# A Mamba cross-attention layer with routed experts: the short convolution on TensorE, and all expert products in plain fp32

## What is computed

```
x   = einsum('ed,bld->bel', in_proj_w, ctx)                 # 256 channels
xc  = depthwise causal conv of x, 4 taps per channel
u   = silu(xc + conv_b)
dt, B, C = split(x_proj_w @ u);  delta = softplus(dt_proj_w @ dt + dt_proj_b)
state = state * exp(delta * A) + (delta * u) * B            # 16 states, 256 steps
y   = (sum over states of state * C + D * u) * silu(layernorm(input))
x1  = input + tanh(g0) * y
h   = silu(hn @ wg[e].T) * (hn @ wu[e].T), hn = layernorm(x1)   # 10 experts, 176 wide
out = x1 + tanh(g1) * (shared + 2.5 * top-2 weighted sum of h @ wd[e].T)
```

## Time and profile before

| | us |
|---|---|
| median of 3 runs (lowest, highest) | 253.39 (253.25, 253.78) |
| the profiled execution | 253.55 |
| its span | 251.7 |
| busy PE, DVE, ACT, POOL | 205.5, 215.0, 171.2, 195.3 |

### The profile page before, as it was taken

One profiled execution on the slowest core, in us unless ns is written; L12 is line 12 of the kernel. 1 busy time (PEld: TensorE's weight loads), 2 busy tenths in 40 slices (PEclk: granted clock), 3 DMA queues, 4 the chain that ended last, 5 costly groups with the idle time before them and its releaser, 6 DMA issues. The chain is left out here.

```text
span 251.7 us, 3757 instructions
## 1 busy us (share of the span) xinstructions
PE 205.5 (82%) x874; PEld 148.7 (59%) x874; DVE 215.0 (85%) x522; ACT 171.2 (68%) x508; POOL 195.3 (78%) x237
## 2 busy tenths in 40 slices
PE   8534594658669895677996899889999999999995
PEld 4223273434355662345854587568888778788884
DVE  2789999999998989999999999989999999645340
ACT  4579879997758997458757998676775682343220
POOL 0248889999999999999999999999999996510000
PEclk9855579575979999999999999999999999999999
DMA  6496999770490202002209302020300000000000
GB/s 183 140 263 172 336 410 321 281 230 1 130 364 12 83 21 87 0 16 68 81 14 329 109 0 83 27 83 3 101 3 0 22 3 3 21 0 0 3 21 21
DMA packets 26821, 25.45 MB, mean 101 GB/s; under 512 B 1064, under 2 KB 25904, under 8 KB 26160
## 3 DMA queue, kind: packets, MB, share of 16 engines
q1 hardware_dynamic: 26512, 25.06, 30.7%
q10 hardware_dynamic: 288, 0.16, 0.2%
HBM read 24.04 MB, written 1.18 MB: 100 GB/s over the span
## 5 line engine op out<-in xcount | busy, mean ns | idle before, releaser
L1061 POOL TENSOR_TENSOR dbu<-du,bb 128x512 f32<-128x512 f32 x64 | 81.3, 1284 | 5.1 <-DVE du L463 3.3
L704 ACT ACTIVATE psA<-delta,aneg 128x127 f32<-128x127 f32 x256 | 78.0, 358 | 5.6 <-DVE psH L953 5.3
L953 DVE TENSOR_TENSOR_SCAN psH<-psA,dbu 128x512 f32<-128x512 f32 x64 | 76.5, 1218 | 1.5 <-POOL dbu L1087 0.4
L667 PE MATMUL psU<-wup,hnT 128*128 128x352 f32 x176 | 63.6, 491 | 12.8 <-DVE hcat L869 8.9
L1104 POOL TENSOR_TENSOR acc<-acc,prod 128x512 f32<-128x512 f32 x42 | 54.5, 1297 | 2.4 <-DVE prod L963 1.8
L545 PE MATMUL psD<-wdn,hT 128*128 128x256 f32 x224 | 52.2, 380 | 0.6 <-issue 0.6
L667 PEld LDWEIGHTS psU<-wup,hnT 128*128 128x128 f32 x176 | 32.8, 200 | 32.8 <-DVE hcat L869 13.6
L833 ACT ACTIVATE tg<-psU 128x176 f32<-128x176 f32 x80 | 24.4, 314 | 36.7 <-PE psU L667 23.9
L545 PEld LDWEIGHTS psD<-wdn,hT 128*128 128x128 f32 x224 | 41.5, 190 | 6.7 <-issue 1.1
L963 DVE TENSOR_TENSOR prod<-psH,cc 128x512 f32<-128x512 f32 x64 | 41.9, 679 | 1.1 <-POOL acc L1104 0.7
L1035 DVE SCALAR_TENSOR_TENSOR ag<-tg,psU 128x176 f32<-128x176 f32 x80 | 25.5, 330 | 15.5 <-ACT tg L833 15.1
(11 more groups left out here) (117 smaller groups left out, 282.9 us busy)
## 6 DMA issues: line engine op xcount, KB each, us to landing
cc<-brows SPq DMA_DIRECT2D x16, 512.0 KB, 4.9
bb<-brows SPq DMA_DIRECT2D x3, 2048.0 KB, 7.6
wup<-in_w_up SPq DMA_DIRECT2D x1, 1760.0 KB, 12.2
wdn<-in_w_down SPq DMA_DIRECT2D x1, 1664.0 KB, 16.5
wup<-in_w_up SPq DMA_DIRECT2D x1, 1408.0 KB, 8.4
x_sb<-in_x SPq DMA_DIRECT2D x4, 256.0 KB, 4.2
bb<-brows SPq DMA_DIRECT2D x1, 1024.0 KB, 5.9
out<-outb SPq DMA_DIRECT2D x8, 128.0 KB, 1.7
```

The source lines that it names most:

```text
L667: last = pe.matmul(dst, hnT[:, b % 2, k, lh * P:(lh + 1) * P], wup[:, j - 1, k, :], start=(k == 0), stop=(k == KT - 1))
L704: last = act.activation(dst[:, j, h, 1:], delta[:, b % 2, h, l0 + 1:l1], ACT.Exp, scale=aneg[:, h * DS + s0 + j:h * DS + s0 + j + 1])
L953: dve.tensor_tensor_scan(psH[:, i % 2], psA[:, i % DA_RING], dbu[:, i % DBU_RING], 0.0, ALU.mult, ALU.add).then_inc(s_scan, 1)
L1061: pool.tensor_tensor(tile(dbu[:, m % DBU_RING], m), du[:, b % 2, :, l0:l1].unsqueeze(1).broadcast_to(shape), bb[:, b % 2, s0:s0 + ns, l0:l ...
```

## The change

The short convolution is made on TensorE: for each of the four taps, `win` is scaled by that tap per channel into `wk[:, k]`, and `project` accumulates four products of shifted context in PSUM. The scaling is done once at the start, two taps on VectorE and two on GpSimd (`scale_tap`), from a broadcast of the taps over all partitions that ScalarE's queue loads into two slots of `prod`. `project_out` scales by 0.5 and adds the bias; `tap0` to `tap2` are gone. All units are plain fp32 products; `whi`, `wlo`, `hnhi`, `hnlo` and the tasks that make them are gone. The orders of all engines but SyncE are written anew.

```diff
@@ the tables of units
-SPLIT = ((1, 2), (3, 3), (5, 2), (7, 3), (9, 2))
...
@@ set-up
+        wk = sb("wk", [P, DC, DI])
-        whi = sb("whi", [P, NSPLIT, KT, 2 * FF], F32R)
-        wlo = sb("wlo", [P, NSPLIT, KT, 2 * FF], F32R)
+        taps = prod[:, 0:2, :].rearrange("p r (k d) -> p (r k) d", d=DI)
-        hnhi = sb("hnhi", [P, 2, KT, P], F32R)
-        hnlo = sb("hnlo", [P, 2, KT, P], F32R)
...
+        def scale_tap(engine, k):
+
+            if k >= 2:
+                engine.wait_ge(d_win, 16)
+                engine.wait_ge(d_taps, 16)
+            engine.tensor_tensor(wk[:, k], win[:, :], taps[:, k], ALU.mult).then_inc(s_wk[k % 2], 1)
...
@@ TensorE, project
-                        pe.wait_ge(d_win, 16)
...
                     for h in range(EH):
-                        last = pe.matmul(dst[:, h, :], win[:, h * P:(h + 1) * P], ctx_sb[:, b, lo:l1],
-                                         start=True, stop=True)
+                        for k in reversed(range(DC)):
+                            back = DC - 1 - k
+                            if i == 0 and h == 0:
+                                pe.wait_ge(s_wk[k % 2], 2 - k // 2)
+                            n0 = max(l0, back)
+                            last = pe.matmul(entry(i)[:, h, n0 - l0:], wk[:, k, h * P:(h + 1) * P],
+                                             ctx_sb[:, b, n0 - back:l1 - back], start=(k == DC - 1), stop=(k == 0))
...
@@ TensorE, up
-                    elif j not in SLOT or t < SPLIT[SLOT[j]][1]:
+                    else:
                         for k in range(KT):
                             last = pe.matmul(dst, hnT[:, b % 2, k, lh * P:(lh + 1) * P], wup[:, j - 1, k, :],
                                              start=(k == 0), stop=(k == KT - 1))
-                    else:
...
-                        for k in range(KT):
-                            h_hi, h_lo = hnhi[:, t % 2, k, :], hnlo[:, t % 2, k, :]
-                            w_hi, w_lo = whi[:, slot, k, :], wlo[:, slot, k, :]
-                            pe.matmul(dst, h_hi, w_hi, start=(k == 0), stop=False)
-                            pe.matmul(dst, h_hi, w_lo, start=False, stop=False)
-                            last = pe.matmul(dst, h_lo, w_hi, start=False, stop=(k == KT - 1))
@@ ScalarE
+            act.dma_start(taps[:, :, :], w_taps.unsqueeze(0).broadcast_to([P, DC, DI])).then_inc(d_taps, 16)
             act.dma_start(win[:, :], w_in).then_inc(d_win, 16)
...
-                        act.activation(xh[:, h, l0:l1], src[:, h, l0 - lo:], ACT.Identity,
-                                       scale=Wh[:, h, DC - 1:DC],
-                                       bias=cwh[:, EH * DC + h:EH * DC + h + 1]).then_inc(s_xh, 1)
+                        act.activation(xh[:, h, l0:l1], entry(i)[:, h, :], ACT.Identity,
+                                       scale=0.5, bias=cwh[:, h:h + 1]).then_inc(s_xh, 1)
...
@@ VectorE
+                    for k in (3, 1):
+                        scale_tap(dve, k)
                     dve.wait_ge(d_par, 16)
...
-                        dve.scalar_tensor_tensor(xh[:, h, n0:l1], src[:, h, n0 - back - lo:l1 - back - lo],
-                                                 Wh[:, h, k:k + 1], xh[:, h, n0:l1],
-                                                 ALU.mult, ALU.add).then_inc(s_tap, 1)
@@ GpSimd
+                if task == "load":
+                    for k in (2, 0):
+                        scale_tap(pool, k)
...
-                    pool.tensor_tensor(hnlo[:, i % 2], hnT[:, b % 2, :, h * P:(h + 1) * P], hnhi[:, i % 2],
-                                       ALU.subtract).then_inc(s_hnlo, 1)
...
-                    pool.tensor_tensor(wlo[:, k], wup[:, SPLIT[k][0] - 1], whi[:, k], ALU.subtract).then_inc(s_wlo, 1)
```

More of the change, by code:

```diff
@@ L143 @@
     "TensorE": """
[L144 to L157, removed]
+        project:0 project:1 xproj:0 dt:0 xproj:1 dt:1 project:2 prod:0 prod:1 prod:2 prod:3 xproj:2 dt:2 prod:4
@@ L158 @@
+        down:23 up:64 up:65 to_tokens:7 up:66 turn:24 up:67 up:68 turn:25 to_features:7 up:69 up:70 turn:26
+        up:71 down:24 up:72 up:73 down:25 up:74 up:75 turn:27 up:76 turn:28 down:26 up:77 down:27 up:78 turn:29
+        up:79 turn:30 down:28 down:29 turn:31 down:30 down:31
     """,
     "ScalarE": """
-        load:0 project_out:0 project_out:1 tanh_u:0 xproj_out:0 tanh_u:1 dt_out:0 soft_exp:0 xproj_out:1
-        soft_log:0 dt_out:1 soft_exp:1 soft_log:1 first:0 scan:0 skip:0 project_out:2 scan:1 scan:2 z_norm:0
@@ L162 @@
[L162 to L165, removed]
-        gate:5 scan:19 scan:20 gate:6 gate:7 hidden:1 scan:21 scan:22 dt_out:3 skip:2 gate:8 gate:9 soft_exp:3
@@ L182 @@
[L182 to L183 removed]
+        load:0 project_out:0 z_norm:0 project_out:1 tanh_u:0 tanh_u:1 xproj_out:0 dt_out:0 soft_exp:0
+        xproj_out:1 soft_log:0 dt_out:1 soft_exp:1 first:0 soft_log:1 scan:0 scan:1 scan:2 skip:0 z_gate:0
+        project_out:2 tanh_u:2 scan:3 scan:4 decay:0 xproj_out:2 scan:5 scan:6 dt_out:2 soft_exp:2 scan:7 scan:8
@@ L187 @@
-        z_stats:3 log_2:0 delta0:0 delta1:0 log_1:1 delta2:0 log_2:1 delta0:1 scan:0 scan:1 delta1:1 keep_ends:0
-        keep_ends:1 tap0:2 prod:0 prod:1 tap1:2 tap2:2 scan:2 scan:3 prod:2 prod:3 keep_ends:2 keep_ends:3
-        silu_u:2 scan:4 delta2:1 scan:5 z_gate:0 keep_ends:4 keep_ends:5 prod:4 prod:5 scan:6 scan:7 prod:6
-        keep_ends:6 keep_ends:7 prod:7 scan:8 scan:9 gate_y:0 prod:8 prod:9 residual:0 log_1:2 stats:0
-        variance:0 scan:10 prod:10 log_2:2 scan:11 scan:12 prod:11 prod:12 tap0:3 tap1:3 scan:13 gate:0 route:0
@@ L212 @@
-        keep_ends:55 gate:49 prod:55 scan:56 z_gate:3 mul:49 gate:50 route:5 mul:50 scan:57 prod:56 prod:57
-        gate:51 gate:52 mul:51 mul:52 scan:58 scan:59 finish:4 gate:53 mul:53 gate:54 mul:54 residual:6 stats:6
-        gate:55 variance:6 mul:55 prod:58 gate:56 mul:56 prod:59 gate:57 mul:57 scan:60 scan:61 gate:58 mul:58
-        gate:59 prod:60 prod:61 scan:62 gate:60 prod:62 mul:59 route:6 mul:60 scan:63 prod:63 gate:61 mul:61
-        gate:62 mul:62 finish:5 gate:63 mul:63 residual:7 gate:64 mul:64 stats:7 variance:7 gate:65 mul:65
+        load:0 z_stats:0 z_stats:1 z_stats:2 z_stats:3 silu_u:0 silu_u:1 log_1:0 log_2:0 delta0:0 delta1:0
@@ new lines @@
+        delta2:0 log_1:1 log_2:1 scan:0 scan:1 prod:0 keep_ends:0 keep_ends:1 prod:1 scan:2 delta0:1 scan:3
+        delta1:1 prod:2 prod:3 keep_ends:2 keep_ends:3 silu_u:2 z_gate:0 scan:4 scan:5 prod:4 keep_ends:4
+        keep_ends:5 prod:5 delta2:1 scan:6 scan:7 prod:6 prod:7 keep_ends:6 keep_ends:7 log_1:2 scan:8 scan:9
+        gate_y:0 prod:8 prod:9 scan:10 scan:11 prod:10 log_2:2 scan:12 residual:0 stats:0 prod:11 variance:0
+        scan:13 prod:12 prod:13 scan:14 scan:15 prod:14 gate:0 route:0 mul:0 gate:1 prod:15 mul:1 silu_u:3
```

193 lines of the change are left out of this document (83 added, 110 removed).

## The result

| | before | after |
|---|---|---|
| median us (lowest, highest) | 253.39 (253.22, 253.78) | 251.71 (250.78, 252.24) |
| ratio, 95% interval | | 0.993 (0.9911 to 0.995) |
| profiled execution, us | 253.55 | 251.53 |
| its span, us | 251.7 | 249.7 |

What follows compares the result with a forecast made beforehand. Bound taken as a scan stage where DVE and POOL hold each other, then a tail of pure PE work. Terms +2.7 - 1.8 - 7.5 + 0.8 + 3.8 = -2.0 from 253.55, less 0.16: 251.4 us, range 248.9 to 255.2.

Steps and rivals of the forecast that it cites:

- Prologue: Before the first scan: taps load and scalings delay it from 18.71 to 21.4 us, +2.7, bounds +1.5 and +4.4.
- rival 3: Long prologue, +4.4 in place of +2.7, as loads share queues and `win` stands behind the taps; 253.1 us, chance 0.13.
- The side question of that term: Prologue: whether DVE's and POOL's scalings exclude each other, ending at 7.9 us one after the other, or at 7.0.
- Stage 18.7 to 40: First scan stage, DVE full: six taps of piece 2 leave DVE, `delta0:1` comes in; -1.8 us, bounds -0.5 and -3.0.
- Stage 40 to the handover: Scan stage until PE's tail: POOL loses 8.2 us, DVE 5.0; -7.5, with +0.8 for PE's wider conv.
- a stall of PE: Scan stage: `project:3` and `project:4` grow to 16 instructions, `gate:0` may wait; +0.8 us, bounds 0 and +4.0.
- POOL would fall to 92%: Sign to look for in the scan stage: POOL's share down to about 92%, DVE's up to 97%.
- Tail, +3.8: PE's last stretch: 21 split units become plain at 1.18 us each, +4.6 less 0.8; bounds +3.6 and +4.6.
- The 0.8 that was taken off for PE's standing: Tail: PE stands 0.98 of 86.0 us, which longer units can fill in part, -0.8 at most.
- Rival 1: Scan stage keeps DVE's gaps, set by order and not POOL's load; stage gives 5.0, 253.9 us, chance 0.17.
- Rival 2: Wide conv on PE's slow clock: DVE stands around `project:2` and `project:3`, 4.0 in place of 0.8; 254.6 us, chance 0.13.
- Rival 4: All gives way: stage from 40 us -8.2, prologue +1.5, no PE stall; 248.7 us, chance 0.14.

## Why the prediction was right

**What bounds the kernel.** Right: a scan stage of DVE and POOL, and a tail of PE. The tail began at 157.43 where 157.4 was forecast, as the sum of terms that were off by +2.3, -0.3 and -2.0.

**Prologue, +2.7, measured +5.0: mis-sized, beyond even the bound of 4.4.** The forecast took `silu_u:0` at 13.0 us from the chain of `z_stats`; that chain ended at 13.45, since `x_sb` was there only at 10.57 and not at 9.7, and PE's chain held `silu_u:0` till 13.88. Its way to the first scan was taken as 8.4 us; it was 9.9. The steps that failed:

- PE's own work was left out of the path. I costed the products at nothing because `z_stats` would end later. They began after a wait of 2.7 us, most of them ran at about half pace, and their chain ended last, by 0.43 us. The upper bound names the lower clock, but the sum does not hold it. Without taps, and with no such wait, the 32 products take 1.9 us less.
- Eleven products of zeros stood ahead of `xproj:0`. They were hidden before, when PE had them done and waited 0.71 us for `u`, as the row of `xproj:0` below shows; now PE was late and they were worth 0.9 us, as the run without them shows.
- The broadcast of the taps held `win` till 6.07, not 5.5, as rival 3 feared.

```profile
8.14 0.60 PE L580 MATMUL psM<-u,wx 128*40 128x128 f32 x4 [0.71 <-DVE u L917]
```

The side question of that term, whether DVE's and POOL's scalings exclude each other, was answered in kind and not in size. The rows that show DVE's two in 1.29 us and POOL's two in 1.82 end at 7.94; DVE's second takes 0.95 us in place of 0.42, POOL's 0.96 and 0.91 in place of 0.73. The Trainium skill, SBUF — State Buffer, "Who interferes with whom", says that such instructions contend, and the trace agrees. But 7.94 beside the 7.9 that I had made of it is luck: the forecast began at 5.5, the scalings at 6.07. They took 1.87 us together, between the 2.4 that I took for one after the other and the 1.5 for POOL alone.

**Stage 18.7 to 40, -1.8, measured -2.1.** Right.

**Stage 40 to the handover, -6.7 together, measured -8.7: the direction right, the size short.** I halved DVE's idle time and added a stall of PE. Of the two, the stall was near (0.50 us where 0.8 was taken). What I had not seen is that the new order is worth more than the taken-off work: in the old order this stage gave -2.6 with the units alone and with the conv it lost 3.2. The forecast that POOL would fall to 92% is wrong, it is at 59.19 of 60 us in the middle of the stage. With the split units back it is as full (59.33 of 60 us) and the handover is 9.3 us later, which fits a bound that stayed where it was, beside a DVE at 108.1 of 112.4 us from 45 us on (14.07 + 57.77 + 36.24), which is 96%.

**Tail, +3.8, measured +3.8,** and +3.6 in the run with this edit alone. Right, with units at 1.18 to 1.19 as forecast. The 0.8 that was taken off for PE's standing is not what the stretches show: PE stands 0.68 of 89.6 us now and 0.98 of 86.0 before, so a longer unit filled 0.3 of it. What took off the other 0.5 is open.

**The rivals.** Rival 3 came true in size (+5.0 for +4.4), and was paid for by the stage. Rival 1's condition, less than 5.5 us from the stage, did not occur. Rival 2's mechanism is real and was measured at 5.05 us of waiting in the old order (0.31 before). The forecast said that the two were close, 8 against 8.5 us, and gave it 0.13; the new order had placed enough of DVE's work there. Rival 4's stage came true, its prologue did not. A fair account: the total was right to 0.3 us, with errors of +2.3 and -2.0 in two parts of its sum, and that they cancelled is luck.

## What to carry to other kernels

Where the order of the work is written out by hand, a change of durations and its order are one change: here each half, and both together in the old order, were slower than before by 0.3 to 5.4%, and a test of an edit in the old order would have thrown away a gain. When weights are first made on the chip, cost the wait of TensorE twice: once for the time it stands, and once for the products that run at the lower clock after it, and look for filler work that was hidden as long as the engine was early. An engine that is the bound does not show slack when it is relieved; look at when its work is done, not at its share.
